# Transposes of the mixed rows: made in the second gather stage instead of the combination stage

## The chip, the cores and the metric

The kernel runs on one core of one Trainium2 chip. The metric is the device time of one execution in microseconds (us); less is better. Three executions of the kernel before took 3115.58, 3129.86 and 3129.86 us, median 3129.86 us.

## What is computed

A graph of 6250 nodes with 256 features and 100,000 edges goes through two layers; everything is float32. The parts that matter here, cut from the reference:

```python
# layer 0, end: two of six experts per node, weighted and added
x = x + ffn0(layernorm(x))                 # h = relu(..), sum over the two chosen experts of weight * expert(h)
xn = layernorm(x)                          # "the mixed rows": one mean and one deviation per node
# layer 1: messages over the edges, and a linear attention over all nodes
s      = xn[edge_src]                      # gather of rows, one per edge
msg    = tensor_product(s, edge_attr) * radial(edge_len_emb)
agg    = segment_sum(msg, edge_dst)        # sums per target node
qkv    = xn @ Wqkv.T                       # 8 heads of 64
k, v   = inst_norm(k), inst_norm(v)        # over the 64 features of a head
dots   = einsum("bhnd,bhne->bhde", k, v)   # summed over all 6250 nodes
mixed  = (q @ dots / n) @ Wout.T + bout
x = x + agg + mixed
x = layer1_ffn(x)                          # then the last stage
```

## The kernel before

The program is a row of phases, each between barriers of all engines. Each engine (PE, which multiplies matrices; DVE, ACT and POOL for vector work; SP, which only issues DMAs) has an instruction list of its own, written out by Python in a fixed order; waits on semaphores tie them together. Two phases are touched.

**The combination stage** (phase p6, second half, about 1575 to 1682 us of the span). The outputs of the experts lie in DRAM (`z_d`, two rows for each node). For each of `NB` = 25 blocks of 250 nodes (two tiles of 125 rows, t = 0 and 1) SP loads four pieces of `z_d` (500 KB in all: four DMAs from `start_rows`, L101). POOL multiplies the first expert's two tiles by their gates (L2082) and adds the residual `x1s` (L2085). DVE adds the second expert's product (`mix`, L2120), takes the statistics (L1468 to L1474), and from ACT's square root (`deviation_of`, L2012) makes reciprocal and shift (`shift_of`, L2130 and L2133). ACT writes the normed rows `xm` in four instructions (`normed`, L2002). SP stores them to `xm_d` (two DMAs, 250 KB). PE then transposes them (`turned`, four matmuls, L2061), ACT copies the result out of PSUM (`copy`, L2008), and SP stores it to `xmT_d` (250 KB, L1967). `pipeline` gives each stage function a lag: in step s an engine does the function of lag k for block s - k, in the order in which the list names them. ACT's list is

```python
pipeline(e, NB, [(copy, 2), (normed, 1), (deviation_of, 0)], loop=False)
```

**The second gather stage** (phase g2, from about 1682 to 2720 us) has 391 groups of 256 edges. For each, POOL issues two indirect DMAs of 128 rows from `xm_d` (`gather`, L2510) into a ring of `GB` = 13 groups; it waits until PE has summed the group that used the slot before. DVE and ACT make one-hot matrices, weighted per edge (`make_hot`, `weigh`). PE multiplies (`sums`, L2157) into PSUM, and DVE adds the PSUM result to a ring of node sums (`accumulate`, L2640). Up to group `ALONE` = 228 two groups share one PSUM bank, and the pairs take the banks 0, 1 and 4 in turn (`bank_of`). `timeline` orders all work by steps: step s has group s on POOL, group s - 5 on PE and so on. Other plans are laid over the groups: `KV` starts every fourth step from step 6, once for each of `NT` = 50 tiles of 125 nodes, and makes keys and values from `xmT_d` (`load_kv` on SP, `project` on PE L2763, `square` on ACT, `size` and `scale_k` on DVE, `products` on PE L2772); `MIX` folds the result into one matrix; `P9` and `F3`, from step 218, read `xmT_d` and the node sums to make the output rows of each tile (`product` and `turned` on PE, `x3_of` and `f3_of` on DVE). `RAD` makes the radial weights in 96 units (PE L2741 and L2753).

`Steps.wait(e, i, name)` makes engine e wait until item i has passed its step `name`; `Landing.wait` does so for DMAs. The other lines named in this document are helpers: L101 is `start_rows`, L1468 to L1474 `row_stats`.

## Time and profile before

| | |
|---|---|
| median of three runs | 3129.86 us (3115.58 to 3129.86) |
| the profiled execution | 3123.76 us |
| its span, first to last instruction | 3122.2 us |
| busy share of the span | PE 85%, POOL 58%, DVE 55%, ACT 46% |
| granted TensorE clock, mean | 0.943 of full speed |

The span is the profiled one; the profiled execution's own time is 1.6 us longer than it. All rows below come from that execution. Times in a row are counted from the span's start. A lower busy share than 100% says little by itself here: each stage has its own limit, so stages are read one by one.

### The profile page before, as it was taken

The numbers are of one execution on the slowest core, as the hardware profiler recorded it, in microseconds if no ns is written. First come the engines' busy times: TensorE is split into PE (matmuls) and PEld (weight loads), VectorE is DVE, ScalarE is ACT, GpSimd is POOL, SyncE is SP. The second block draws the span as 40 slices with busy tenths as digits, with TensorE's granted clock in tenths as the row PEclk, the third lists the DMA queues.
The fourth block names the chain that finished last, engine by engine and source line by source line (L and its number), as shares of the span: only waits on it lengthen the run. The fifth ranks groups of instructions, "written<-read, shape, count | busy, mean of one in ns | idle before, by whom it ended". The sixth has DMA issues, their size and how long they took to land. (4 is left out here: it accounts for less than half of the span.)

```text
span 3122.2 us, 54248 instructions
## 1 busy us (share of the span) xinstructions
PE 2645.5 (85%) x14909; PEld 2211.8 (71%) x14909; DVE 1716.8 (55%) x5340; ACT 1446.5 (46%) x4046; POOL 1819.7 (58%) x1962
## 2 busy tenths in 40 slices
PE   1999998998998996899934899899887888689998
PEld 1777778787887885788822666666677777578886
DVE  7733335777775667333364556566566667533333
ACT  4022222552233553333346988787576766322221
POOL 5777777777773355244476777777777777200000
PEclk9999999999999998899955999999999999799999
DMA  7364446767774774333276444444466655422222
GB/s 225 114 191 142 137 139 190 226 214 221 219 229 138 227 225 153 89 95 95 85 217 212 116 126 116 125 117 124 124 181 177 174 161 162 131 73 73 68 66 55
DMA packets 291701, 464.78 MB, mean 149 GB/s; under 512 B 91221, under 2 KB 224276, under 8 KB 290074
## 3 DMA queue, kind: packets, MB, share of 16 engines
q1 hardware_dynamic: 207804, 232.37, 25.1%
q0 software_dynamic: 81216, 221.98, 24.3%
q10 hardware_dynamic: 2402, 7.19, 0.7%
q8 instruction: 115, 1.88, 0.2%
q14 instruction: 164, 1.34, 0.1%
HBM read 349.16 MB, written 112.23 MB: 148 GB/s over the span
## 5 line engine op out<-in xcount | busy, mean ns | idle before, releaser
L2510 POOL DMA_INDIRECT g_got<-xm_d,idx x782 | 762.7, 975 | 253.5 <-issue 216.4
L886 POOL DMA_INDIRECT g_got<-xn_d,idx x702 | 684.8, 975 | 231.7 <-issue 211.9
L2157 PEld LDWEIGHTS ps<-g_hotw,g_got 128*128 128x128 f32 x3128 | 401.1, 196 | 168.8 <-DMA g_got<-xm_d,idx 89.0
L2157 PE MATMUL ps<-g_hotw,g_got 128*128 128x128 f32 (+11 forms) x3128 | 423.1, 285 | 95.9 <-DMA g_got<-xm_d,idx 66.6
L1279 PEld LDWEIGHTS ps<-g_hot,g_got 128*128 128x128 f32 x2808 | 354.0, 195 | 79.3 <-DMA g_got<-xn_d,idx 39.4
L1279 PE MATMUL ps<-g_hot,g_got 128*128 128x120 f32 (+4 forms) x2808 | 369.3, 279 | 34.2 <-DMA g_got<-xn_d,idx 26.5
L2559 ACT ACTIVATE g_hotw<-g_hot,g_wr 128x16 f32<-128x16 f32 (+8 forms) x1308 | 300.3, 308 | 86.7 <-DVE g_hot L598 86.4
L1479 POOL TENSOR_TENSOR p_ln_rs<-p_ln_pre,neg_half 125x2 f32<-125x2 f32 x50 | 35.2, 705 | 510.3 <-DVE p_ln_pre L1474 510.3
L2640 DVE TENSOR_TENSOR g_ring<-g_ring,ps 128x84 f32 (+10 forms) x391 | 133.5, 341 | 308.1 <-PE ps L2157 170.2
L2073 POOL DMA_INDIRECT z_d<-p_yj,p_to x108 | 122.1, 1130 | 205.7 <-DVE p_to L2106 183.8
L2960 ACT ACTIVATE p_hid<-ps,p_b 128x250 f32<-128x250 f32 x200 | 82.9, 466 | 278.5 <-PE ps L2922 278.5
L2037 PE MATMUL ps<-gin_hid,p_wj 128*128 128x256 f32 x864 | 197.4, 382 | 1.3 <-ACT gin_hid L1979 0.8
L2939 PE MATMUL ps<-p_w,p_hid 128*125 128x256 f32 x800 | 179.2, 382 | 22.2 <-ACT p_hid L2960 22.2
L1688 PE MATMUL ps<-gin_w,gin_hid 128*125 128x256 f32 x800 | 188.6, 385 | 9.1 <-POOL p_before L1747 9.1
L1418 PE MATMUL ps<-g_hT,g_w 128*128 128x250 f32 x800 | 190.8, 383 | 4.6 <-DVE g_hT L1105 4.6
L1093 DVE TENSOR_TENSOR g_ring<-g_ring,ps 128x40 f32 (+9 forms) x351 | 74.0, 211 | 217.0 <-PE ps L1279 125.4
L2922 PE MATMUL ps<-p_f3T,p_w 128*128 128x250 f32 x800 | 175.0, 375 | 12.8 <-DMA p_w<-in_L_ffn_W 12.8
L2939 PEld LDWEIGHTS ps<-p_w,p_hid 128*125 128x125 f32 x800 | 148.2, 188 | 52.9 <-ACT p_hid L2960 30.2
L2763 PE MATMUL ps<-g_half 128*125 128x512 f32 x400 | 184.9, 606 | 0.0
L2037 PEld LDWEIGHTS ps<-gin_hid,p_wj 128*128 128x128 f32 x864 | 165.1, 191 | 24.5 <-issue 1.1
L1988 ACT ACTIVATE gin_hid<-ps,p_wj 128x256 f32<-128x256 f32 x216 | 90.7, 471 | 188.6 <-PE ps L2037 188.6
L2922 PEld LDWEIGHTS ps<-p_f3T,p_w 128*128 128x128 f32 x800 | 151.3, 189 | 32.5 <-issue 12.9
(376 smaller groups left out, 5039.7 us busy)
## 6 DMA issues: line engine op xcount, KB each, us to landing
h_d<-gin_hid SPq DMA_DIRECT2D x23, 1000.0 KB
gin_hid<-h_d SPq DMA_DIRECT2D x23, 1000.0 KB
p_xr<-jobs_d SPq DMA_DIRECT2D x54, 258.0 KB, 2.8
g_got<-xm_d,idx POOLq DMA_INDIRECT x782
g_half<-xmT_d SPq DMA_DIRECT2D x100, 125.0 KB
g_got<-xn_d,idx POOLq DMA_INDIRECT x702
p_wj<-z_d SPq DMA_DIRECT2D x50, 224.0 KB
q_d<-g_qo SPq DMA_DIRECT2D x25, 250.0 KB
```

Of the source, the lines that this page charges most:

```text
L886: landed.start(e.indirect_dma_start(got[:, k % (2 * GB), :], None, xn_d[0:N, :], bass.IndirectOffsetOnAxis(ap=idx[:, HT + k:HT + k + 1], a ...
L1279: mm = e.matmul(to, got[:, 2 * (g % GB) + j, c * P:(c + 1) * P], hot[:, g % HR, j, 0:w].unsqueeze(1).broadcast_to([P, r, w]), start=(j == ...
L1418: mm = e.matmul(ps[:, 5 + n % 2, k * BN:(k + 1) * BN], w1[:, c, f:f + P], hT[:, i % 2, c, :], start=(c == 0), stop=(c == DC - 1))
L1688: mm = e.matmul(ps[0:TN, i % 2, t * D:(t + 1) * D], hid[:, slot(i), c, t * TN:(t + 1) * TN], w2[:, c, :], start=(c == 0), stop=(c == HC - 1))
L2037: mm = e.matmul(ps[:, 2 * k + u, o * JOB:(o + 1) * JOB], w[:, c, o * P:(o + 1) * P], src[:, u, c, :], start=(c == 0), stop=(c == DC - 1))
L2157: mm = e.matmul(to, rows[j][:, c * P:(c + 1) * P], hotw[:, j, c * w:4 * w].unsqueeze(1).broadcast_to([P, r, n]), start=(j == 0), stop=(j = ...
L2510: landed.start(e.indirect_dma_start(got[:, 2 * (g % GB) + j, :], None, xm_d[0:N, :], bass.IndirectOffsetOnAxis(ap=idx[:, 2 * g + j:2 * g + ...
L2559: ins = e.activation(hotw[:, u, 1, m * w:(m + 1) * w], hot[:, u, 1, 0:w], ACT.Copy, scale=chunk(n)[:, k, m:m + 1])
L2640: added.done(e.tensor_tensor(to, to, sums_of(bank_of(g)[0], w, bank_of(g)[1]), ALU.add), "add")
L2763: mm = e.matmul(ps[0:TN, bank, :], kT[:, i % 2, c, :], wkv[:, c, at:at + INNER], start=(c == 0), stop=(c == DC - 1))
L2922: mm = e.matmul(ps[:, q, m * BN:(m + 1) * BN], w1[:, k, c, f * P:(f + 1) * P], f3T[:, u, :, c * TN:(c + 1) * TN], start=(c == 0), stop=(c ...
L2939: mm = e.matmul(ps[0:TN, 4 + u, t * D:(t + 1) * D], hid[:, u, k, f, t * TN:(t + 1) * TN], w2[:, k, f, :], start=(j == 0), stop=(j == 2 * F ...
```

## The change

In the combination stage PE's `turned`, ACT's `copy` and SP's `store_T` go away, with their buffer and waits. ACT takes one of POOL's two gate products (`gate_first`, tile t = 0), and ACT's functions get larger lags. In the second gather stage a key and value step first loads the 125 rows of a tile from `xm_d` into `kr` (two slots that lie in `mix1`, which is written only later), PE transposes them (`turn_k`, into PSUM bank `XT` = 4), DVE copies them to `kT` (`copy_k`), and SP stores `kT` to `xmT_d` for the later readers (`store_kT`). All later steps of `KV` get two steps more of lag, `MIX` begins two steps later, and the shared banks are 0 and 1 only.

```diff
@@ combination stage
-                    pipeline(e, NB, [(load_z, 0), (store, ZB - 1), (store_T, ZB)], loop=False)
+                    pipeline(e, NB, [(load_z, 0), (store, ZB - 1)], loop=False)
...
-                        mturn.wait(e, i - AB, "turn")
                         m_out.wait(e, r, i // AB - 1)
...
-                    def copy(i, u, h):
-                        mturn.wait(e, i, "turn")
-                        t_out.wait(e, i % AB, i // AB - 1)
-                        mcopied.done(e.activation(xmT[:, i % AB, :], ps[:, 6 + u, 0:2 * BN], ACT.Copy), "T")
+                    def gate_first(i, u, h):
+                        z_in.wait(e, i % ZB, i // ZB)
+                        gated.done(e.activation(acc[:, i % AB, 0, :], z[:, i % ZB, 0, 0, :], ACT.Copy,
+                                                scale=gates[:, 2 * i, 0:1]), "g0")
...
-                    pipeline(e, NB, [(copy, 2), (normed, 1), (deviation_of, 0)], loop=False)
+                    pipeline(e, NB, [(normed, 3), (deviation_of, 2), (gate_first, 0)], loop=False)
...
-                    def turned(i, u, h):
-                        ln.norm.wait(e, i, "v1")
-                        mcopied.wait(e, i - 2, "T")
...
-                    pipeline(e, NB, [(turned, 0)], loop=False)
...
-                        for t in range(2):
-                            first.done(e.tensor_scalar(acc[:, i % AB, t, :], z[:, i % ZB, 0, t, :],
-                                                       gates[:, 2 * i + t, 0:1], None, ALU.mult), f"g{t}")
+                        first.done(e.tensor_scalar(acc[:, i % AB, 1, :], z[:, i % ZB, 0, 1, :],
+                                                   gates[:, 2 * i + 1, 0:1], None, ALU.mult), "g1")
                         first.wait(e, i, "g1")
+                        gated.wait(e, i, "g0")
@@ second gather stage
+            kr = mix1[0:TN, :, :]
...
-            MIX = [KV[-1] + 13]
+            MIX = [KV[-1] + 15]
...
-                return (FREE[g % 4], 0) if g >= ALONE else ((0, 1, 4)[g // 2 % 3], g % 2 * D)
+                return (FREE[g % 4], 0) if g >= ALONE else (g // 2 % 2, g % 2 * D)
...
                     def load_kv(i):
-                        proj.wait(e, i - 2, "v")
-                        k_in.start(e.dma_start(kT[:, i % 2, :, :],
-                                               xmT_d[i // 2].rearrange("p (c t n) -> p c t n", c=DC, t=2)[:, :, i % 2, :]),
-                                   i % 2)
+                        kturn.wait(e, i - 2, "T")
+                        k_in.start(e.dma_start(kr[:, i % 2, :], tile_of(xm_d, i)), i % 2)
+
+                    def store_kT(i):
+                        kcopy.wait(e, i, "T")
+                        k_out.start(e.dma_start(xmT_d[i // 2].rearrange("p (c t n) -> p c t n", c=DC, t=2)[:, :, i % 2, :],
+                                                kT[:, i % 2, :, :]), i % 2)
...
-  SP    (KV, [(load_kv, 0)])
+  SP    (KV, [(store_kT, 4), (load_kv, 0)])
-  ACT   (KV, [(square, 5), (roots, 8)])
+  ACT   (KV, [(square, 7), (roots, 10)])
-  DVE   (KV, [(scale_k, 9), (size, 6)])
+  DVE   (KV, [(scale_k, 11), (size, 8), (copy_k, 3)])
-  PE    (KV, [(products, 11), (project, 3)])
+  PE    (KV, [(products, 13), (project, 5), (turn_k, 2)])
...
+                    def copy_k(i):
+                        kturn.wait(e, i, "T")
+                        proj.wait(e, i - 2, "v")
+                        k_out.wait(e, i % 2, i // 2 - 1)
+                        kcopy.done(e.tensor_copy(kT[:, i % 2, :, :], ps[:, XT, 0:DC * TN].rearrange("p (c n) -> p c n", c=DC)), "T")
...
+                    def turn_k(i):
+                        k_in.wait(e, i % 2, i // 2)
+                        kcopy.wait(e, i - 1, "T")
+                        for c in range(DC):
+                            mm = e.transpose(ps[:, XT, c * TN:(c + 1) * TN], kr[:, i % 2, c * P:(c + 1) * P], ident[0:TN, 0:TN])
+                        kturn.done(mm, "T")
```

The four lines that begin with an engine's name are cut from the `timeline` calls. `project` waits for `kcopy` of its tile where it waited for `k_in`. SP's first `load` of `P9` also waits for the last stores of `kT`.

How the instructions stand now, at three places. First ACT in the middle of the combination stage, one block and the start of the next, before (`p_dev` is the square root, `p_xm` the normed rows, `p_xmT` the copy of the transposes):

```order
893 L2012 ACTIVATE p_dev<-p_ln_pre 125x2
894 L2008 ACTIVATE p_xmT<-ps 128x500
895 L2002 ACTIVATE p_xm<-p_acc,p_shift,xm_rs 125x64
896 L2002 ACTIVATE p_xm<-p_acc,p_shift,xm_rs 125x64x3
897 L2002 ACTIVATE p_xm<-p_acc,p_shift,xm_rs 125x64
898 L2002 ACTIVATE p_xm<-p_acc,p_shift,xm_rs 125x64x3
```

and ACT there in the changed kernel (L1998 is `gate_first`):

```order
889 L2003 ACTIVATE p_dev<-p_ln_pre 125x2
890 L1998 ACTIVATE p_acc<-p_wj,gates 125x256
891 L1993 ACTIVATE p_xm<-p_acc,p_shift,xm_rs 125x64
892 L1993 ACTIVATE p_xm<-p_acc,p_shift,xm_rs 125x64x3
893 L1993 ACTIVATE p_xm<-p_acc,p_shift,xm_rs 125x64
894 L1993 ACTIVATE p_xm<-p_acc,p_shift,xm_rs 125x64x3
```

The copy, which waits for PE, has given its place to a product that waits only for a DMA. Second, PE in the second gather stage, one key and value step in steady running, before (each `x2` of `ps<-g_hotw,g_got` is half of a group's sums; L2772 `products`, L2763 `project`):

```order
1220 L2753 MATMUL ps<-g_w1b,g_embT 128x512
1221 L2741 MATMUL ps<-ident,g_emb 80x128
1222 L2157 MATMUL ps<-g_hotw,g_got 128x128 x2
1223 L2157 MATMUL ps<-g_hotw,g_got 128x120 x2
1224 L2772 MATMUL ps<-g_half 128x128 x4
1225 L2763 MATMUL ps<-g_half 125x512 x4
1226 L2157 MATMUL ps<-g_hotw,g_got 128x128 x2
```

and PE in the changed kernel (L2752 is `turn_k`, L2771 and L2762 are `products` and `project`):

```order
1198 L2771 MATMUL ps<-g_half 128x128 x4
1199 L2762 MATMUL ps<-g_half 125x512 x4
1200 L2135 MATMUL ps<-g_hotw,g_got 128x128 x2
1201 L2135 MATMUL ps<-g_hotw,g_got 128x120 x2
1202 L2752 MATMUL ps<-ident,g_mix 128x125 x2
1203 L2135 MATMUL ps<-g_hotw,g_got 128x128 x2
1204 L2135 MATMUL ps<-g_hotw,g_got 128x120 x2
```

Two transposes stand behind a group's sums, one step after `project` of the tile before. Third, SP in the second gather stage, before:

```order
973 L588 DMA g_emb<-in_edge_attr 128x1280
974 L2468 DMA g_half<-xmT_d 128x2x125 x16
975 L588 DMA g_emb<-in_edge_attr 128x1280
976 L2468 DMA g_half<-xmT_d 128x2x125 x16
977 L588 DMA g_emb<-in_edge_attr 128x1280
```

and SP in the changed kernel (L2449 is `load_kv`, L2453 `store_kT`):

```order
970 L2449 DMA g_mix<-xm_d 125x256
971 L588 DMA g_emb<-in_edge_attr 128x1280
972 L2453 DMA xmT_d<-g_half 256x1x125
973 L2449 DMA g_mix<-xm_d 125x256
974 L2453 DMA xmT_d<-g_half 256x1x125
975 L2449 DMA g_mix<-xm_d 125x256
```

Each load now stands behind the store of the tile before, which waits for DVE's copy; before, the loads waited only for `project` two tiles back.

## Rows read from the trace of the kernel before

**Rows 1.** Page: the chain that ended last by engine, and a costliest group.

```profile
issue 16%; PE 12%; POOL 7%; DVE 5%; DMA 2%; DVEq 2%; ACT 1%; SPq 0%; POOLq 0%; ACTq 0%
...
L2510 POOL DMA_INDIRECT g_got<-xm_d,idx x782 | 762.7, 975 | 253.5 <-issue 216.4
```

**Rows 2.** Tile g_got: durations ns min/median/max, first and last start.

```profile
L2510 POOL DMA_INDIRECT g_got<-xm_d,idx x782: 942/949/2623, 1682.5 to 2682.4; - x196
```

**Rows 3.** Waits of POOL, 1700 to 2200 us: total, times, longest.

```profile
POOL g_got L2510 <- issue: 112.5, 369, 0.3
POOL g_got L2510 <- PE ps L2157: 7.0, 23, 0.3
```

**Rows 4.** Tile g_got from 1682 to 2495 us, POOL and PE.

```profile
L2510 POOL DMA_INDIRECT g_got<-xm_d,idx x635: 942/949/2623, 1682.5 to 2494.8; - x159
...
L2157 PE MATMUL ps<-g_hotw,g_got x2448: 232/275/582, 1693.5 to 2494.1; 128*128 128x96 f32 x47, 128*128 128x128 f32 x37, 128*128 128x120 f32 x27, 128*128 128x108 f32 x22
```

**Rows 5.** Timeline of the combination stage: start, length, instruction, idle before.

```profile
1587.78 1.85 ACT L2002 ACTIVATE p_xm<-p_acc,p_shift,xm_rs 125x64 f32<-125x64 f32 x4 [1.25 <-DVE p_shift L2133]
...
1589.57 1.09 DVE L2120 SCALAR_TENSOR_TENSOR p_acc<-p_wj,gates,p_acc 125x256 f32<-125x256 f32 x2
...
1592.10 0.72 DVE L1474 TENSOR_SCALAR p_ln_pre<-xm_mv 125x2 f32<-125x2 f32 x1
...
1626.48 1.85 ACT L2002 ACTIVATE p_xm<-p_acc,p_shift,xm_rs 125x64 f32<-125x64 f32 x4
...
1626.94 2.09 SPq L101 DMA_DIRECT2D p_wj<-z_d  x4
...
1628.38 1.09 PE L2061 MATMUL ps<-ident,p_xm 125*128 125x125 f32 x4 [2.42 <-ACT p_xm L2002]
...
1629.51 0.59 ACT L2008 ACTIVATE p_xmT<-ps 128x500 f32<-128x500 f32 x1 [0.68 <-PE ps L2061]
...
1629.99 1.85 ACT L2002 ACTIVATE p_xm<-p_acc,p_shift,xm_rs 125x64 f32<-125x64 f32 x4
...
1669.44 0.17 DVE L1474 TENSOR_SCALAR p_ln_pre<-xm_mv 125x2 f32<-125x2 f32 x1
...
1672.96 1.84 ACT L2002 ACTIVATE p_xm<-p_acc,p_shift,xm_rs 125x64 f32<-125x64 f32 x4
1674.83 0.79 SPq L101 DMA_DIRECT2D xm_d<-p_xm  x2
...
1675.66 1.28 SPq L1967 DMA_DIRECT2D xmT_d<-p_xmT  x2
```

**Rows 6.** Tile p_acc: POOL's product and sum.

```profile
L2082 POOL TENSOR_SCALAR p_acc<-p_wj,gates x50: 918/927/1223, 1579.8 to 1664.8; 125x256 f32<-125x256 f32 x50
...
L2085 POOL TENSOR_TENSOR p_acc<-p_acc,store x25: 1261/1265/1277, 1581.7 to 1665.9; 125x512 f32<-125x512 f32 x25
```

**Rows 7.** Window of the stage: busy us, then clock, DMA share, GB/s.

```profile
1620.00:1640.00 20.00, 6.01 (x23) 4.08 (x24) 16.16 (x48) 13.43 (x34) 17.95 (x18) 0.50 0.94 291
```

**Rows 8.** Tile g_gw: ACT, 125x256 with a scale per row.

```profile
L949 ACT ACTIVATE g_gw<-g_wn,ones,g_rr x50: 584/590/602, 518.3 to 959.6; 125x256 f32<-125x256 f32 x50
```

**Rows 9.** PE in 1700 to 2200 us, by line: busy, mean ns, idle before.

```profile
L2157 PE MATMUL ps<-g_hotw,g_got 128*128 128x96 f32 (+5 forms) x1593 | 204.4, 278 | 35.8 <-DMA g_got<-xm_d,idx 32.5 <-ACT g_hotw L2559 3.0
```

**Rows 10.** Chain at 1750 to 1759 us, a transpose in PE's row.

```profile
1758.63 0.11 PE ps L2741
```

**Rows 11.** DMA issues: KB each, us to landing.

```profile
f3T_d<-g_f3T SPq DMA_DIRECT2D x50, 125.0 KB, 4.0
```

**Rows 12.** Timeline of the second gather stage: gathers beside two DVE instructions.

```profile
1695.94 2.29 DVE L2593 SCALAR_TENSOR_TENSOR g_half<-g_means,g_half 128x2048 f32<-128x2048 f32 x1
1696.43 2.62 POOL L2510 DMA_INDIRECT g_got<-xm_d,idx  x1 [0.30 <-issue]
...
2232.94 1.23 DVE L2676 COPY g_a<-ps 128x1024 f32<-128x1024 f32 x1 [4.35 <-PE ps L2780]
2233.26 0.95 POOL L2510 DMA_INDIRECT g_got<-xm_d,idx  x1 [0.30 <-issue]
```

More of the change, by code:

```diff
@@ L1930, in gps_kernel @@
             ysum = ph.steps("ysum", "y")
-            first = ph.steps("first", "g0", "g1", "a")
+            gated = ph.steps("gated", "g0")
+            first = ph.steps("first", "g1", "a")
             mixed = ph.steps("mixed", "b0", "b1")
@@ L2391, in gps_kernel @@
             folded = ph.steps("folded", "pad")
-            k_in = ph.landing("k", 2)
+            k_in, k_out = ph.landing("k", 2), ph.landing("kT", 2)
+            kturn = ph.steps("kturn", "T")
+            kcopy = ph.steps("kcopy", "T")
             proj = ph.steps("proj", "k", "v")
@@ L2483, in load @@
                             dots.wait(e, NT - 1, "dots")
+                            for u in range(2):
+                                k_out.wait(e, u, (NT - 1 - u) // 2)
                         rows.wait(e, i - XI, "rows")
@@ L2574, in _ @@
                     timeline(LAST_STEP, (GROUPS, [(weigh, 3)]), (RAD, [(do_silu, 7), (copy_emb, 3)]), (ZERO, [(zero, 0)]),
-                             (KV, [(square, 5), (roots, 8)]), (PAIRS, [(deviations, 9)]), (F3, [(copy, 2)]))
+                             (KV, [(square, 7), (roots, 10)]), (PAIRS, [(deviations, 9)]), (F3, [(copy, 2)]))
                 @block.vector
```

27 lines of the change are left out of this document (5 added, 22 removed).

## The prediction

> **What bounds the kernel now.** I read the chain that ended last first. It shares 16% to "issue", 12% to PE and 7% to POOL [rows 1], so no engine holds the whole kernel and each stage has to be read alone. The change touches two stages, the combination stage and the second gather stage.
>
> The second gather stage is bound by POOL's gathers. POOL issues 782 of them from 1682.5 to 2682.4 us [rows 2], one every (2682.4 - 1682.5) / 781 = 1.28 us: 0.975 us for the DMA instruction itself, and a gap that "issue" explains nearly always [rows 1]. From 1700 to 2200 us POOL waited for PE 23 times, never over 0.3 us, which is also the gap of a gather that waits for nobody [rows 3]. The reader should see in this that POOL never stalls there. The ring holds 13 groups, and POOL stalls only when PE is 13 groups behind. How near that comes is seen from two counts at one time: at 2495 us POOL had issued 635 gathers, 317.5 groups, and PE had finished 2448 / 8 = 306 groups (eight records for each), so PE was 11.5 groups behind [rows 4]. That is near the tightest place, with 1.5 groups of room, 1.5 x 2.56 = 3.8 us. So work that is added for PE, DVE or ACT in this stage costs nothing until PE falls 13 groups behind, and the stage as a whole moves with POOL's first gather.
>
> POOL's first gather comes when the combination stage has ended and its rows have landed. So each microsecond that the combination stage loses is lost from the total.
>
> That stage has a period for each block of 250 rows. ACT's first normed block begins at 1587.78 us, its 25th at 1672.96 [rows 5]: 85.18 / 24 = 3.55 us. What ends the period is a loop between ACT and PE that nothing overlaps: ACT norms (1.85 us), PE transposes what was just written (1.09 us and the way to it), ACT copies (0.59 us), and norms again, 1626.48 to 1629.99 us, 3.51 us [rows 5]. POOL is close behind with two products and a sum, 2 x 0.93 + 1.27 = 3.13 us [rows 6], and so is the DMA: its share was 0.94 at 291 GB/s [rows 7], so it is busy for 0.94 x 3.53 = 3.3 us of each block. Three resources at 3.1 to 3.5 us is why one edit alone could not have gained much here; the change relieves all three.
>
> **The change, term by term.**
>
> *The period of the combination stage.* After the change the limits for a block are these.
> - ACT: norms 1.85 us [rows 5], square root 0.20 (estimate, a 125x2 instruction), one product of 125x256 with a scale per row, 0.59 us [rows 8], and about 0.1 of gaps: 2.7 us.
> - POOL: 0.93 + 1.27 us [rows 6]: 2.2, with gaps 2.3 us.
> - DVE: from the start of the second product, 1589.57, to the start of the last small instruction, 1592.10, are 2.53 us [rows 5], plus that instruction. It took 0.17 us with POOL idle and 0.72 with POOL at work [rows 5]. So 2.70 to 3.25 us.
> - DMA: 750 of 1000 KB stay (two reads of 250 KB and one write; a second write goes). By bytes 3.3 x 0.75 = 2.5 us, and at the same 0.94 share 2.65.
> - SP: four loads took 2.09 us to issue and two stores 0.79 [rows 5]: 2.9 us. This was hidden under 3.5; now it is among the longest.
> - A loop over two blocks: ACT's product, POOL's sum 1.27, DVE's product pair 1.09, reciprocal and shift about 0.45, ACT's norms 1.85, square root 0.20, ACT's next product 0.59, and six hand-overs of about 0.03: 5.6 / 2 = 2.8 us.
>
> ACT now waits for `z_d` itself, with the norms of an earlier block queued behind it. The loads of block i + 1 stand on SP behind the store of block i - 4: 0.79 + 2.09 us of issue, 2.5 to 4 us to land (the nearest row, a 125 KB store, says 4.0 [rows 11]), product 0.6, norms 1.9, over three blocks: 2.6 to 3.1 us. I take 2.9 us, at SP's own time and in the middle of the last loop. Gain 24 x (3.55 - 2.9) = 15.6 us. The ends are 2.7 us (20.4) and 3.26 (7.0), if DVE is held up in every block.
>
> On DVE's small instruction a rule bears. The row says that it lasted 0.72 us beside POOL and 0.17 without. The Trainium skill (SBUF — State Buffer, section "SBUF: two separate sides") says that VectorE and GpSimd share a port pair as an exclusive lock held for a whole instruction, in place of each sharing the bandwidth. By that rule the small instruction ends when POOL's sum ends, whereupon DVE's next product may start anyway, and the period follows the loop's 2.8 us; by the row at its worst it would be 3.25.
>
> *The start of that stage.* POOL makes one product of 0.93 us [rows 6] for a block where it made two. ACT's first norms stand behind the sums of two blocks: 2 x 0.93 = 1.9 us earlier.
>
> *Its end.* The last norms end at 1674.80. The last issue of SP ends at 1675.66 + 1.28 = 1676.94 now, and at 1674.83 + 0.79 = 1675.62 without the transposed rows [rows 5]: 1.3 us. What follows (landing, barrier, loads) is unchanged.
>
> *Transposes in the second gather stage.* Two for each of 50 tiles. A transpose in a row of matmuls advances the chain by 0.11 us [rows 10], so 0.22 us per tile. A tile takes four groups, 4 x 2.56 = 10.2 us of POOL's time, 49 tiles in 1700 to 2200 us: 10.8 us of new work, and PE's idle time before the sums alone was 35.8 us there [rows 9]. Even at the 0.278 us of one whole matmul record in that row it would be 27 us, still less. Cost 0. In the combination stage the granted clock is 0.50 already [rows 7], so PE's idling there loses nothing new.
>
> *`copy_k` on DVE.* The nearest row is a copy out of PSUM of 1024 columns in 1.23 us [rows 12]; by columns 0.30 us for 250, 15 us in all, against 1.23 each (61 us) as the upper bound. DVE mostly waits for PE in this stage. Cost 0. It could hurt POOL instead: one DVE instruction with both inputs in SBUF stretched the gather beside it to 2.62 us, whereas the gather beside the copy out of PSUM took its usual 0.95 [rows 12]. I take the second, 0; the first is a rival below.
>
> *The load and store of each tile.* 125 KB in and 125 KB out, every 10.2 us. Each load now waits for the copy of the tile before. From PE's transposes the way is: copy 0.3, SP's two issues 0.8, landing up to 4.0 [rows 11], transposes 0.2: some 5.5 us of 10.2. SP has nothing else but three large loads of `g_emb` in this stretch; a load behind one of them may be late by some us, which PE's room takes. Cost 0.
>
> *Two shared banks for three.* A pair's bank is wanted again three steps after its last sum, and DVE's two additions stand one step before. PE has 2 steps of about 2.5 us, DVE needs under 1 us. Cost 0.
>
> *`P9` two steps later.* The first 27 tiles come later, the 28th by one step, the rest at their old steps. The dense part ends one step later, at the tight place of rows 4. With 3.8 us of room I put 1 us of stall there, between 0 and 5.
>
> **Sum.** 15.6 + 1.9 + 1.3 - 1 = 17.8 us off. The profiled execution's own time was 3123.8 us, 6.1 under the median of the three runs: 3106 us.
>
> **The rivals.**
> - *The forecast*, a gain of 14 to 24 us: 0.60, of which 0.02 at the low end count as within 0.5%.
> - *The combination stage is held by what stays* (SP's issue, loads that land late, DVE behind POOL), period 3.1 to 3.4 us: 24 x 0.3 + 3.2 - 1 = 9 us off, 3114 us. For it speaks that three loops lie within 0.3 us of each other, against it that each one by itself fits in 2.9. 0.23.
> - *The copies stretch gathers.* If each of the 50 held up a gather for its own 0.3 to 0.43 us, 15 to 21 us come back: 3121 to 3127 us. Rows 12 speak against it. 0.07.
> - *The transposing loop outlasts four groups* (the slower side). Copy, store, load, landing and transposes have 10.2 us. Each tile's excess is counted 50 times: 0.36 us eats the gain, and from 0.67 us, a loop of 10.9 us, the kernel is slower by over 0.5%; at 12 us it is 90 us, less 33 us that the ring's room takes, less 18: 3163 us. The in-order queues speak for it (SP's load behind a wait for DVE, DVE's copy behind a wait for PE), the 5.5 us against. 0.10.
>
> About 0.5%, 16 us, is what a measurement of this kernel can tell from no change; the three runs before lie 14 us apart. Faster by more: 0.58. Within: 0.02 + 0.23 + 0.07 = 0.32. Slower: 0.10.
>
> The range goes down to 3094: a gain of 23 us at the 2.7 us period, and 7 us of scatter of the runs. It goes up to 3124, which takes in the second rival, and most of the third. What is left out is the slower rival and the far ends: 2 in 10.
>
> **What the profile would show.** Starts of ACT's norms 2.9 us apart, and the first gather at about 1664 in place of 1682.5. POOL's gathers still 1.28 us apart, with no wait over 0.3 us, and the last one 1000 us after the first. A transpose pair in the second gather stage that adds 0.2 us to PE's row, with waits for the load of `kr` rare. The prediction is wrong if norms come over 3.2 us apart, if gathers beside `copy_k` last longer than 0.95 us, or if POOL waits for PE's sums from 1700 us on.

## The result and the profile after

The changed kernel takes 3111.06 us (median of 20 runs, 3103.31 to 3116.28), the kernel before 3123.59 us on the same chip (20 runs, 3114.24 to 3129.86). The ratio is 0.996, with a 95% interval of 0.995 to 0.997: 12.5 us less. The prediction was 3106 us, in a range of 3094 to 3124. Two later executions, of 3718 us (e4) and 5550 us (e8), were in a slower state and are left out of all medians. The profiled execution of the changed kernel took 3110.37 us, its span is 3108.8; rows of before are those of its profiled execution, span 3122.2.

The page first: the chain that ended last by engine, and the costliest group (busy, mean ns of one, idle before).

```profile
issue 16%; PE 12%; DVE 6%; POOL 6%; DVEq 2%; DMA 2%; ACT 1%; SPq 0%; POOLq 0%; ACTq 0%
...
L2496 POOL DMA_INDIRECT g_got<-xm_d,idx x782 | 763.9, 977 | 250.7 <-issue 215.7
```

It reads like [rows 1]; at this scale nothing has changed. The gathers of the second gather stage, with the tile's durations, first and last start, and the sums that follow them:

```profile
L2135 PE MATMUL ps<-g_hotw,g_got x3128: 232/275/609, 1674.4 to 2685.4; 128*128 128x128 f32 x62, 128*128 128x96 f32 x38, 128*128 128x176 f32 x20, 128*128 128x80 f32 x19
...
L2496 POOL DMA_INDIRECT g_got<-xm_d,idx x782: 942/946/2846, 1664.1 to 2664.9; - x196
```

The first gather is at 1664.1 us (forecast about 1664; 1682.5 in [rows 2]). From first to last are 1000.8 us, against 999.9. POOL's waits in the stretch that [rows 3] has, moved with the stage (1681 to 2182 us; total, times, longest):

```profile
POOL g_got L2496 <- issue: 111.5, 366, 0.3
POOL g_got L2496 <- PE ps L2135: 7.9, 26, 0.3
```

No wait is over 0.3 us, so POOL never stalls here either. The transposes and their copy, by line in the same stretch:

```profile
L2638 DVE COPY g_half<-ps 128x250 f32<-128x250 f32 x49 | 20.5, 418 | 59.0 <-PE ps L2752 58.9
L2752 PE MATMUL ps<-ident,g_mix 125*128 125x125 f32 x98 | 18.5, 270 | 0.0
```

49 tiles cost PE 18.5 us (0.38 a tile: forecast 0.22, with 0.28 a transpose as the upper bound) and DVE 20.5 (0.42 a tile, forecast 0.30). PE never stood idle ahead of a transpose, so the load of `kr` was never late there.

The combination stage, as a timeline (start, length, engine, idle before):

```profile
1584.47 1.86 ACT L1993 ACTIVATE p_xm<-p_acc,p_shift,xm_rs 125x64 f32<-125x64 f32 x4 [1.46 <-DVE p_shift L2111]
...
1586.78 1.86 ACT L1993 ACTIVATE p_xm<-p_acc,p_shift,xm_rs 125x64 f32<-125x64 f32 x4
...
1590.47 1.86 ACT L1993 ACTIVATE p_xm<-p_acc,p_shift,xm_rs 125x64 f32<-125x64 f32 x4 [1.46 <-DVE p_shift L2111]
...
1607.44 0.49 ACT L1998 ACTIVATE p_acc<-p_wj,gates 125x256 f32<-125x256 f32 x1
...
1608.08 1.26 POOL L2063 TENSOR_TENSOR p_acc<-p_acc,store 125x512 f32<-125x512 f32 x1 [0.15 <-ACT p_acc L1998]
1608.26 1.10 DVE L2111 SCALAR_TENSOR_TENSOR p_shift<-xm_mv,xm_rs 125x2 f32<-125x2 f32 x1
...
1609.40 1.87 ACT L1993 ACTIVATE p_xm<-p_acc,p_shift,xm_rs 125x64 f32<-125x64 f32 x4 [1.46 <-DVE p_shift L2111]
...
1611.69 0.16 DVE L2111 SCALAR_TENSOR_TENSOR p_shift<-xm_mv,xm_rs 125x2 f32<-125x2 f32 x1
...
1654.91 1.86 ACT L1993 ACTIVATE p_xm<-p_acc,p_shift,xm_rs 125x64 f32<-125x64 f32 x4 [0.44 <-DVE p_shift L2111]
```

The 25 norms start from 1584.47 to 1654.91: 70.44 / 24 = 2.94 us each, where [rows 5] gave 3.55. They don't come evenly: 2.31 and 3.69 us lie between the first three. The shift of 125x2 lasts 0.16 us alone, but at 1608.26, beside POOL's sum, 1.10; ACT's norm waits behind it. The sum ends at 1609.34, the shift at 1609.36.

The waits of that stage (1573 to 1662 us) name four suspects for the 2.94 us, the loads ahead of POOL and of ACT, the shift, and ACT's product:

```profile
POOL p_acc L2059 <- DMA p_wj<-z_d: 16.6, 17, 6.0
ACT p_acc L1998 <- DMA p_wj<-z_d: 16.6, 10, 11.7
ACT p_xm L1993 <- DVE p_shift L2111: 12.5, 19, 1.6
...
POOL p_acc L2063 <- ACT p_acc L1998: 5.0, 7, 1.5
```

Most turns go by the loads. One round of that loop, from ACT's norms of one block over SP's store and its next load (that of the block five later) to ACT's product of that block and the norms behind it:

```profile
1611.88 1.87 ACT L1993 ACTIVATE p_xm<-p_acc,p_shift,xm_rs 125x64 f32<-125x64 f32 x4 [0.26 <-DVE p_shift L2111]
...
1613.93 0.82 SPq L101 DMA_DIRECT2D xm_d<-p_xm  x2
...
1614.79 1.80 SPq L101 DMA_DIRECT2D p_wj<-z_d  x4
...
1619.80 0.51 ACT L1998 ACTIVATE p_acc<-p_wj,gates 125x256 f32<-125x256 f32 x1 [0.39 <-DMA p_wj<-z_d]
...
1620.44 1.85 ACT L1993 ACTIVATE p_xm<-p_acc,p_shift,xm_rs 125x64 f32<-125x64 f32 x4
```

The norms at its end are those of the block three later: 8.56 / 3 = 2.85 us a block. The next round, from the norms at 1614.34 to those at 1623.49 us, takes 3.05 a block. ACT's norms wait 1.4 us or more for the shift in only 4 of the 24 turns.

The window (busy us of PE, PEld, DVE, ACT, POOL; granted clock, DMA share, GB/s) shows none of them full. DVE comes nearest with 18.24 of 20 us, in which the time that it is held is counted. The DMA fell from the 0.94 and 291 of [rows 7]:

```profile
1620.00:1640.00 20.00, 0.00 (x0) 0.00 (x0) 18.24 (x63) 16.81 (x42) 16.26 (x14) 0.50 0.90 267
```

**Where the time came from.** From the first load of `z_d` to the first gather are 91.2 us (1572.85 to 1664.09), against 107.0 (1575.52 to 1682.53): 15.8 us less. Of these 14.7 are the period (85.2 less 70.4 us), 0.6 the start (load to first norm 11.6, against 12.3), 0.4 the end (last norm to first gather 9.2, against 9.6). The stages ahead ended 2.7 us earlier, which the change doesn't touch. Against this stand 1.0 us in the gathers and 4.1 us from the last gather to the end of the span (443.9, against 439.8). 15.8 + 2.7 - 1.0 - 4.1 = 13.4 us, the difference of the two spans. The medians, which don't hold the scatter of one execution, give 12.5.

### The profile page after: what moved, and what is told of

Same layout as the page of the kernel before. It is cut to its first block and busy times, and to the rows that moved or that the text cites. A ratio compares the mean times of both kernels' runs of the same rounds, so it can differ in the third digit from the quotient of the medians.

```text
span 3108.8 us, 54377 instructions
## 1 busy us (share of the span) xinstructions
PE 2628.5 (85%) x14909; PEld 2210.4 (71%) x14909; DVE 1731.9 (56%) x5390; ACT 1451.0 (47%) x4048; POOL 1794.1 (58%) x1937
## 5 line engine op out<-in xcount | busy, mean ns | idle before, releaser
L2496 POOL DMA_INDIRECT g_got<-xm_d,idx x782 | 763.9, 977 | 250.7 <-issue 215.7
L2921 PE MATMUL ps<-p_f3T,p_w 128*128 128x250 f32 x800 | 175.2, 375 | 13.4 <-DMA p_w<-in_L_ffn_W 13.4
L2762 PE MATMUL ps<-g_half 128*125 128x512 f32 x400 | 184.0, 603 | 0.0
L1980 ACT ACTIVATE gin_hid<-ps,p_wj 128x256 f32<-128x256 f32 x216 | 90.7, 471 | 188.3 <-PE ps L2028 188.3
```

The lines of the kernel that those rows point to most:

```text
L2496: landed.start(e.indirect_dma_start(got[:, 2 * (g % GB) + j, :], None, xm_d[0:N, :], bass.IndirectOffsetOnAxis(ap=idx[:, 2 * g + j:2 * g + ...
L2762: mm = e.matmul(ps[0:TN, bank, :], kT[:, i % 2, c, :], wkv[:, c, at:at + INNER], start=(c == 0), stop=(c == DC - 1))
L2921: mm = e.matmul(ps[:, q, m * BN:(m + 1) * BN], w1[:, k, c, f * P:(f + 1) * P], f3T[:, u, :, c * TN:(c + 1) * TN], start=(c == 0), stop=(c ...
```

## The experiments

The runs of this part fell on four other chips. On these every kernel is slower: the kernel before takes 3584 us on chip B, 3549 on C, 3551 on D and E (A is the chip above). So each kernel is compared with the kernel before on its own chip, and that chip's trace says what is different. "PE sets the pace" stands in the expectations for chips B to E, where POOL is seen to pause; the last part says how much of this was true.

| kernel | chip | median us | ratio to before (95%) | norm period | `z_d` load to first gather | first to last gather | ring waits |
|---|---|---|---|---|---|---|---|
| before | A | 3123.6 | | 3.55 | 107.0 | 999.9 | 0 |
| after | A | 3111.1 | 0.996 (0.995 to 0.997) | 2.94 | 91.2 | 1000.8 | 0 |
| e1_gate_only | B | 3581.5 | 0.9991 (0.9977 to 1.0006) | 3.51 | 106.1 | 1227.2 | 11 |
| e2_copy_later | B | 3578.5 | 0.999 (0.9977 to 1.0002) | 3.38 | 103.9 | 1227.7 | 10 |
| e3_no_gate | B | 3593.9 | 1.0038 (1.0024 to 1.0052) | 3.21 | 98.5 | 1238.5 | 16 |
| e4_store_later | B | 3581.3 | 0.9993 (0.9975 to 1.001) | 2.96 | 90.7 | 1242.9 | 17 |
| e5_both | C | 3576.5 | 1.0076 (1.0053 to 1.0098) | 3.52 | 106.6 | 1222.3 | 19 |
| e7_two_banks | C | 3564.4 | 1.0039 (1.0023 to 1.0055) | 3.59 | 108.5 | 1226.2 | 15 |
| e8_split_sum | C | 3543.9 | 0.9982 (0.9966 to 0.9998) | 2.77 | 85.8 | 1228.8 | 16 |
| e9_after_again | C | 3550.3 | 1.0004 (0.9991 to 1.0018) | 2.90 | 90.5 | 1227.3 | 17 |
| e10_bank_shared | D | 3547.8 | 0.9981 (0.9965 to 0.9998) | 2.85 | 89.2 | 1220.2 | 12 |
| e11_best | D | 3539.1 | 0.9964 (0.9948 to 0.998) | 2.75 | 85.6 | 1216.0 | 11 |
| e12_before_again | D | 3557.2, one run | | 3.54 | 107.7 | 1209.7 | 8 |
| e13_best_again | E | 3536.8 | 0.9949 (0.9931 to 0.9967) | 2.66 | 84.3 | 1217.3 | 14 |

The period is the last start of ACT's norms less the first, by 24. The fifth to seventh number are from each kernel's one profiled execution. A ring wait is a gap of POOL over 0.45 us ahead of a group's first gather that ends within 1 us of PE's last sum for the group 13 before, counted in the trace. The stages ahead, whose code is the same in all, scatter too: on one chip the combination stage begins up to 16 us earlier in one execution than in another (1776.8 us in e7, 1792.7 in e8). So a total can't be made up from the stages of one execution.

**The combination stage: what held it before, what holds it now.** The first four kernels were to tell this.

`e1_gate_only`: the kernel before, with Scalar's product added.

```diff
+                    def gate_first(i, u, h): ...   # as in the change, POOL keeps one product
-                    pipeline(e, NB, [(copy, 2), (normed, 1), (deviation_of, 0)], loop=False)
+                    pipeline(e, NB, [(copy, 4), (normed, 3), (deviation_of, 2), (gate_first, 0)], loop=False)
```

> The kernel before with only the gate product moved to ACT; the transposes, ACT's copy and the store of the transposed rows stay in the combination stage. The product stands behind the square root, in the time in which ACT waits for PE (1.18 us, of which 0.2 are used). Theory (the loop of norms, transposes and copy sets the period of 3.55 us): the starts of the norms stay 3.5 us apart and the time is that of before within 3 us. Rival (POOL's two products and a sum, or the z loads, set it): 3.2 to 3.3 us apart and 5 to 8 us faster. The second gather stage is that of before: its length from the first gather to the end is one more sample of what before gives (1439.6 us).

The period stays at 3.51 us in every block, though POOL has 0.93 us less to do. Its timeline:

```profile
1831.42 1.10 PE L2067 MATMUL ps<-ident,p_xm 125*128 125x125 f32 x4 [2.42 <-ACT p_xm L2003]
1832.55 0.59 ACT L2009 ACTIVATE p_xmT<-ps 128x500 f32<-128x500 f32 x1 [0.82 <-PE ps L2067]
1833.03 1.84 ACT L2003 ACTIVATE p_xm<-p_acc,p_shift,xm_rs 125x64 f32<-125x64 f32 x4
...
1834.93 1.10 PE L2067 MATMUL ps<-ident,p_xm 125*128 125x125 f32 x4 [2.42 <-ACT p_xm L2003]
```

Norm, transpose, copy, norm: 1831.42 to 1834.93 is one turn of the loop, 3.51 us, and the added product lies in ACT's wait. The loop that the prediction named is the bound of before; the next run opens it.

`e2_copy_later`: the kernel before, with the copy one block later, so that ACT norms a block while PE transposes the last.

```diff
-                    pipeline(e, NB, [(copy, 2), (normed, 1), (deviation_of, 0)], loop=False)
+                    pipeline(e, NB, [(copy, 3), (normed, 1), (deviation_of, 0)], loop=False)
```

> The kernel before with one number changed: ACT copies the transposes one block later (lag 3 in place of 2), so that it no longer waits for PE. All the work and all the bytes stay. Theory (that loop sets the period, POOL at 3.25 and the DMA at 3.3 us are next): norms 3.25 to 3.35 us apart, 5 to 7 us faster than before. Rival (the DMA at a share of 0.94 is already the limit): no change. From the first gather to the end 1439.6 us as before, if this stretch does not scatter.

The period falls to 3.38 us, mostly 3.1 to 3.6 from block to block, where 3.25 to 3.35 was expected. The transfers are next: from 1835 to 1855 us the DMA share is 0.98 at 302 GB/s, and at that rate the 1.02 MB of a block take 3.4 us. By this sum the transposes could not have stayed at 2.94. The kernel that would test it, this edit together with Scalar's product, was not run.

`e3_no_gate`: the kernel after, with both products on POOL.

```diff
-                        first.done(e.tensor_scalar(acc[:, i % AB, 1, :], z[:, i % ZB, 0, 1, :], ...), "g1")
+                        for t in range(2):
+                            first.done(e.tensor_scalar(acc[:, i % AB, t, :], z[:, i % ZB, 0, t, :], ...), f"g{t}")
-                    pipeline(e, NB, [(normed, 3), (deviation_of, 2), (gate_first, 0)], loop=False)
+                    pipeline(e, NB, [(normed, 1), (deviation_of, 0)], loop=False)
```

> The changed kernel with both gate products on POOL again; the transposes stay in the second gather stage. Theory (POOL is then the longest, 0.93 + 0.93 + 1.27 and gaps): norms 3.2 to 3.3 us apart, so about 7 us of the changed kernel's gain are lost, some 5 to 6 us faster than before. Rival (what holds the changed kernel at 2.93 us is the loads and not the engines, and the product on ACT is worth nothing): norms 2.9 to 3.0 us apart, 12 us faster. From the first gather to the end: 1444.7 us in the changed kernel's profile against 1439.6 before; if the 5 us belong to the moved transposes this run shows 1443 or more, if they are scatter it can show 1440.

The period is 3.26 us in nearly every block, and POOL has no gap in it:

```profile
1832.46 1.26 POOL L2057 TENSOR_TENSOR p_acc<-p_acc,store 125x512 f32<-125x512 f32 x1
1833.70 1.94 POOL L2054 TENSOR_SCALAR p_acc<-p_wj,gates 125x256 f32<-125x256 f32 x2
...
1835.72 1.27 POOL L2057 TENSOR_TENSOR p_acc<-p_acc,store 125x512 f32<-125x512 f32 x1
```

So the move of the transposes alone gives 0.3 us a block, and Scalar's product the other 0.3. Neither gives 0.6 alone (e1: 0.03). The time missed its expectation: in place of 5 to 6 us faster, this kernel is 0.38% slower than before (0.24 to 0.52%). What it loses in the second gather stage is taken up below.

`e4_store_later`: the kernel after, with SP's store behind one more load, which gives the loads of a block more time.

```diff
-                    pipeline(e, NB, [(load_z, 0), (store, ZB - 1)], loop=False)
+                    pipeline(e, NB, [(load_z, 0), (store, ZB)], loop=False)
```

> The changed kernel with SP's store of the mixed rows one block later, so that each load of z stands ahead of one store more that waits for ACT's norms. Theory (the loop over SP: norms, store, load, landing, product holds the period at 2.93 us, with spacings that alternate from 2.3 to 4.2): norms 2.6 to 2.75 us apart, 4 to 7 us faster than the changed kernel, 17 to 19 us than before, waits of ACT and POOL for the z loads nearly gone. Rival (DMA share 0.9 is the limit): 2.9 us apart, no change against the changed kernel.

Behind the first block all waits for the loads are gone. What is left from 1805 to 1870 us:

```profile
ACT p_xm L1993 <- DVE p_shift L2111: 16.7, 12, 1.6
POOL p_acc L2063 <- ACT p_acc L1998: 16.2, 13, 1.8
```

and the period is what it was, 2.96 us, now nearly all in turns of 2.31 and 3.68. The 2.6 to 2.75 us that I expected did not come. This doesn't clear the loads in the kernel after, where POOL waits for them 17 times; it shows that a second limit of nearly the same length stands right behind them. The timeline shows that one:

```profile
1841.72 1.26 POOL L2063 TENSOR_TENSOR p_acc<-p_acc,store 125x512 f32<-125x512 f32 x1
1841.91 1.09 DVE L2111 SCALAR_TENSOR_TENSOR p_shift<-xm_mv,xm_rs 125x2 f32<-125x2 f32 x1
...
1843.03 1.86 ACT L1993 ACTIVATE p_xm<-p_acc,p_shift,xm_rs 125x64 f32<-125x64 f32 x4 [1.46 <-DVE p_shift L2111]
...
1845.15 0.16 DVE L2111 SCALAR_TENSOR_TENSOR p_shift<-xm_mv,xm_rs 125x2 f32<-125x2 f32 x1
...
1845.41 1.26 POOL L2063 TENSOR_TENSOR p_acc<-p_acc,store 125x512 f32<-125x512 f32 x1 [1.53 <-ACT p_acc L1998]
```

In every second block DVE's shift starts just behind POOL's sum and lasts as long as that does. ACT, which waits for the shift, comes late to its next product, and POOL's next sum waits for that product. From one sum to the next that way is 1841.72 to 1845.41, the 3.69 us of the long turn: held shift 1.3, norms 1.86, product 0.49. With the shift free the turn takes 2.31. The two together are the prediction's loop over two blocks, 5.6 us by its sum and 5.99 measured. Here ACT's norms wait 1.4 us or more for the shift in 11 of the 24 turns; in the kernel after it is 4, and 2 in e9, which has the same stage. That the loop over the loads and this one come out at nearly the same period is chance.

`e8_split_sum`: both limits relieved. The kernel after, the store as in e4, and POOL's sum in two, so that each is shorter and one stands ahead of the wait for Scalar.

```diff
                         first.wait(e, i, "g1")
+                        first.done(e.tensor_tensor(acc[:, i % AB, 1, :], acc[:, i % AB, 1, :],
+                                                   x1s[:, 2 * i + 1, :], ALU.add), "a1")
                         gated.wait(e, i, "g0")
-                        first.done(e.tensor_tensor(acc[:, i % AB, :, :], acc[:, i % AB, :, :],
-                                                   x1s[:, 2 * i:2 * i + 2, :], ALU.add), "a")
+                        first.done(e.tensor_tensor(acc[:, i % AB, 0, :], acc[:, i % AB, 0, :],
+                                                   x1s[:, 2 * i, :], ALU.add), "a")
```

> The kernel after with POOL's sum over two tiles split in two (the one for its own product made at once, the other when Scalar's product is there), and the store one step later on SP. Theory: the period of 2.94 us is held by a loop over two blocks that contains POOL's sum of 1.26 us, and by DVE's shift, which lasts 1.1 us when it meets that sum; a sum of 0.65 us shortens both, so the period comes to 2.6 to 2.75 us and the stage ends 4 to 8 us earlier than in the kernel after (ratio to it 0.998). Rival: the period is DMA or SP's issue; then it stays at 2.9 us. If two short locks meet DVE as often as a long one, it stays too.

The norms now come every 2.64 us in 15 of the 24 steps, 2.77 on the mean (2.75 and 2.66 in the two later runs). The tile of the shift: durations in ns, minimum, median, maximum.

```profile
L2113 DVE SCALAR_TENSOR_TENSOR p_shift<-xm_mv,xm_rs x25: 160/491/565, 1803.3 to 1870.0; 125x2 f32<-125x2 f32 x25
```

Its longest is 0.57 us, where the kernel after had 1.20 (1.10 on this chip). The stage is 4.7 us shorter than in the unchanged kernel after on the same chip (85.8, against 90.5 us). The median is 6.3 us lower; by the ratios it is 0.22%, with an uncertainty of about as much. The split sum without the later store was not run, so the share of each edit is not known. What holds the turns of 2.64 us now is POOL. The window from 1806 to 1822 us (as above) and POOL's work for one block in it:

```profile
1806.00:1822.00 16.00, 0.00 (x0) 0.00 (x0) 14.71 (x55) 13.40 (x37) 15.50 (x19) 0.50 0.90 262
...
1815.00 0.92 POOL L2059 TENSOR_SCALAR p_acc<-p_wj,gates 125x256 f32<-125x256 f32 x1
1816.01 0.97 POOL L2062 TENSOR_TENSOR p_acc<-p_acc,store 125x256 f32<-125x256 f32 x1
1816.94 0.72 POOL L2065 TENSOR_TENSOR p_acc<-p_acc,store 125x256 f32<-125x256 f32 x1
```

The two sums take 1.69 us where the whole one took 1.26, and with the product that is 2.61 of the 2.64 us. SP has no room left either: from its store at 1808.36 to that at 1819.23 us it issues without a wait, 2.72 us a block.

**The second gather stage: is what was put there free?** On chip A it was, to 1 us. On chip B, e3 and e4 gain 8 and 15 us against e1 in the combination stage and give them back: their gathers last 11 to 16 us longer than in e1 and e2, which keep the stage of before. This lies in the ring waits: their time beyond the usual gap is 32 and 30 us in e1 and e2, 46 and 49 in e3 and e4. Four kernels took the stage's edits apart.

`e7_two_banks` is the kernel before with one line of the change:

```diff
-                return (FREE[g % 4], 0) if g >= ALONE else ((0, 1, 4)[g // 2 % 3], g % 2 * D)
+                return (FREE[g % 4], 0) if g >= ALONE else (g // 2 % 2, g % 2 * D)
```

> The kernel before with only two shared PSUM banks for the early sums, nothing else. Theory: two banks cost nothing, first to last gather within 1 us of the kernel before on the same chip, ratio 1.000 within 0.001. Rival: with two banks PE waits for DVE's two additions at each pair of groups; then PE loses up to 0.3 us for each of some 100 pairs and, where PE sets the pace, 10 us or more show (ratio 1.003), and the transposes are free.

`e5_both` has the combination stage of before and the second gather stage of after, so that the transposes are made twice (in the first for nothing); `e9_after_again` is the kernel after.

> The combination stage of the kernel before with the second gather stage of the kernel after: the transposes are made in both. Theory: the second gather stage's part costs nothing where POOL's gathers set its pace (first to last gather 1000 us, ratio 1.000 within 0.001), and where PE sets it, its 50 tiles cost 11 to 16 us, 0.2 to 0.3 us of PE for each tile (ratio 1.003 to 1.0045). Rival: the part costs nothing on PE either and the 11 to 15 us seen between the kernels were the ending of the combination stage at another moment; then the ratio is 1.000 everywhere.

> The kernel after, unchanged, as the base for the other three on their chip. Where POOL sets the second gather stage's pace: ratio 0.996 to the kernel before. Where PE sets it: 16 us are gained in the combination stage and 11 to 16 lost in the second gather stage, ratio 0.998 to 1.001, as the run with the later store (0.9993) showed.

`e12_before_again` is the kernel before.

> The kernel before, unchanged, for its profile on the chip of these runs. Theory: first to last gather as in the run with three banks shared, norms every 3.51 to 3.55 us, and no waits of the sums for DVE's additions where PE sets the pace. Rival: its gather stage is as long as that of the kernels with two banks; then the time that these lose is elsewhere.

The two banks alone cost 0.39% (14 us, 8 to 20), with PE's work unchanged; here the rival held. No kernel with three banks was profiled on chip C, so where the 14 us are lost can only be read from PE's waits on two chips, from 1950 to 2700 us. The kernel before (e12, chip D):

```profile
PE ps L2157 <- issue: 52.5, 55, 2.6
```

With two banks (e7, chip C):

```profile
PE ps L2157 <- DVE g_ring L2640: 54.3, 19, 7.3
PE ps L2157 <- DVE g_hot L598: 49.6, 23, 4.4
```

The kernel after (e9, chip C):

```profile
PE ps L2135 <- DVE g_hot L598: 56.8, 30, 7.0
PE ps L2135 <- DVE g_ring L2626: 27.6, 13, 4.2
```

With three banks the sums in this stretch wait for nothing of DVE's. With two, they wait 104 and 84 us for its additions (`g_ring`) and for its one-hot matrices, which stand behind the additions in DVE's order. POOL's ring waits rise from 8 to 11 (e1, e2, e12) to 15 to 19 (all kernels with two banks). But these lines tell for whom PE waited last, and not what the banks cost: all of PE's idle time, from 30 us after the first gather to the last one, is 238 us in e12, 248 in e2 and 258 in e1, which have three banks, and 248 in e9 and 262 in e7, which have two. In the kernels with three banks much of it stands under "issue". So that two banks cost time is shown, and that they do it through DVE's order is likely.

What the transposes add is not settled. e5 is slower than e7 by 12 us at the medians, and slower than before by 0.76%, where 0.3 to 0.45% was expected. But e9's combination stage is 16 us shorter than e5's (90.5, against 106.6) and its median is 1.4 us over that of before, so that its second stage costs some 17 us by that count, where e5 says 27 (19 to 35). And from the first gather to the end of the span the profiled execution of e5 is no longer than that of e7 (1672.4, against 1673.6 us).

`e10_bank_shared`: the kernel after, with three banks for the sums, and the transposes in the bank of the keys.

```diff
-            XT, KB, V, DOTS = 4, 3, 5, 6
+            KB, V, DOTS = 3, 5, 6
+            XT = KB
-                return (FREE[g % 4], 0) if g >= ALONE else (g // 2 % 2, g % 2 * D)
+                return (FREE[g % 4], 0) if g >= ALONE else ((0, 1, 4)[g // 2 % 3], g % 2 * D)
 ...
+                        squares.wait(e, i - 1, "raw")        # in turn_k
-            MIX = [KV[-1] + 15]
+            MIX = [KV[-1] + 13]
-                             (KV, [(products, 13), (project, 5), (turn_k, 2)]), ...
+                             (KV, [(products, 11), (project, 4), (turn_k, 2)]), ...
```

with `square`, `roots`, `scale_k` and `size` back at their steps of before.

> The kernel after, but the early sums keep their three PSUM banks, and the transposes of a tile share bank 3 with its key result (project one step after copy_k instead of two, turn_k waits for the squares of the tile before; the dense part keeps its step of before). Theory: what the second gather stage loses where PE sets its pace is the third bank (waits of the sums for DVE, 73 to 104 us in 750 us with two banks, none with three), not the transposes. Then first to last gather returns to that of the kernel before within 3 us, no such waits, and the gain of the combination stage shows in the total: ratio 0.995. Where POOL sets the pace the ratio is 0.995 to 0.996 as well. Rival: the transposes and their copy on DVE cost it themselves; then the span stays 11 to 15 us longer and the ratio is 0.999 to 1.0. A second rival: with one bank for transposes and keys PE waits for Scalar's squares once per tile, and it is slower than the kernel before.

The largest waits of PE from 1950 to 2700 us:

```profile
PE ps L2135 <- issue: 30.2, 37, 1.9
PE ps L2754 <- ACT g_half L2520: 19.4, 12, 3.4
```

The sums' waits for DVE are gone, and a wait of the transposes for Scalar's squares is new, as the second rival said, but it came 12 times and not once per tile, and the kernel is not slower. The gathers last 1220.2 us, 10.5 more than in e12 on the same chip, so the transposes with their copy, load, store and waits cost something there even with three banks, as far as one execution of each can tell. They are 7 us shorter than in e9, but on another chip, and e1 and e12, whose second stage is the same, differ by 17.5 us from chip to chip. The ratio, 0.9981, lies between theory (0.995) and rival (0.999 to 1.0). It is 8 us better than e9's 1.0004, with an uncertainty as large: how much the third bank gave back is not shown.

`e11_best` is e10 with the split sum and the later store; `e13_best_again` is the same kernel.

> The kernel of the run before with POOL's split sum and the later store. Each gain adds to the other: 24 x 0.15 to 0.2 = 4 to 5 us less than that kernel, ratio to before 0.993 to 0.994. Rival: the combination stage's last 4 us lie behind something else, then the ratio equals that kernel's.

> The kernel with the split sum, the later store and three banks once more, as it is. If POOL sets the pace of the second gather stage on this chip (first to last gather near 1000 us): norms every 2.7 to 2.8 us, ratio to before 0.993 to 0.995, and the time from the last gather to the end tells of the 4 us that the kernel after lost there: 440 us if the dense part's later steps were the reason, 444 us if they were not. If PE sets the pace (near 1215 us): ratio 0.995 to 0.998, as on the other such chip.

They take 3539.1 us on chip D (12.3 less than before there) and 3536.8 on E (13.9 less): ratios 0.9964 and 0.9949. The gain of e11 was to be 0.6 to 0.7% and is 0.36% (0.20 to 0.52). The kernel after showed no gain on C and, with the later store, none on B. So this version is faster than before on both chips, where the kernel after was not on its two; the two kernels were never run on the same chip, and on chip A, where POOL doesn't pause, this one was not run at all. Chip E pauses like the other three, so e13 can't tell of the 4 us at the end of the gathers, for which it was also run.

## Why the prediction was right, and where not

- *Direction, size and range*: right. The forecast was 17.8 us off, of which 12.5 came; the range held.
- *The bound of the combination stage before* (the loop of ACT and PE, 3.51 us): shown by e1, where POOL had less to do and nothing moved, and e2, where the loop was opened and the period fell.
- *Its period after*, 2.9 us for a gain of 15.6: measured 2.94 and 14.7. I took it "at SP's own time and in the middle of the last loop", that is from SP and the landing of loads. The loop over the loads is there in most turns, with 2.85 and 3.05 us in the two rounds above, where I had 2.6 to 3.1. SP's own time was sized too large: its store and loads take 0.82 + 1.80 = 2.62 us, not 2.9, and SP waits 17.7 us for ACT's norms in the stage. It is a limit only in e8. What I missed is a second limit of the same length: the loop over two blocks (my 2.8) comes to 2.96 with DVE's shift held behind POOL's sum. It sets 4 of the 24 turns here, and every second one once e4 had taken the waits for the loads away. I had named the hold on DVE as a term for its own busy time ([rows 5], 0.72 us); it acts through ACT, which waits for the shift. So the number rests on the right loop for most turns, and that the other one does not make it longer is luck.
- *The two readings of [rows 5]*: the rule's was the better. The Trainium skill (SBUF — State Buffer, section "SBUF: two separate sides") has the port pair as an exclusive lock, held for a whole instruction. This trace agrees for POOL's sum: all five shifts that began during a sum ended 0.02 us after it (1609.36 and 1609.34 for one), and so did 12 of 12 in e4. So did the 13 small instructions of L1474 that began during one, though they read one tensor only. But beside POOL's product, which reads one tensor too, ten shifts lasted 0.16 to 0.24 us and ended 0.44 us ahead of the product; there the whole instruction was not waited for.
- *The start*, 1.9 us: 0.6. The saved products were there: counted from the first load of `z_d`, the first shift begins 1.56 us earlier (1583.27 less 1572.85, against 1587.50 less 1575.52). But it lasts 1.17 us beside POOL's sum, where before it lasted 0.24, and 0.6 is left.
- *The end*, 1.3 us: 0.4. The issues came as forecast: SP's last ends 2.7 us after the last norms' start (1657.59 less 1654.91), where it was 4.0. From there to the first gather it is 6.5 us now and was 5.6, so "what follows is unchanged" was the wrong half. The store of `xm_d` is now the last one, but that alone is not the reason: it is the last one in e4, e8 and e11 too, and there it is 5.6 to 5.7 us (6.5 in e3, e9, e10 and e13). The cause stays open.
- *Transposes, copy, load and store at no cost; no stretched gathers*: on chip A shown right. The gathers have a median of 0.946 us, beside `copy_k` too, and no gap of POOL between two of them is over 0.32 us. The stage lasts 1.0 us longer, but not by the stall at the tight place for which I had put down 1 us: the gathers themselves take 763.9 us in place of 762.7. That term was right by luck. The room of 3.8 us that I took from the count in [rows 4] was too large. At the closest, PE's sums ended 3.0 us ahead of the gather that reuses their slot before, and end 0.8 us ahead of it now. On chips B to E 0.8 us is also the least that is seen where POOL does wait, so once, at 2469 us, the reserve was used up.
- *Two banks at no cost*: right on chip A (from 1900 us on PE waits 17.6 us for `g_ring`, against 12.9), wrong on C. The step "PE has 2 steps of about 2.5 us, DVE needs under 1 us" counts DVE's own time, not its order. Where DVE is held up by something else, two banks bind PE to it within two steps; this fits the waits of e7, but was not tested by itself.
- *A term that was missing*: PE's lag at the end of the gathers. I let added work be free as long as POOL doesn't stall, but what PE is behind when the last gather is issued comes after it. The last sums end 20.8 us after the last gather began, against 15.8 before, and the end of the span comes 4.1 us later after it. This rests on one execution each. On chips B to E the time from last gather to end is 446.9 to 451.8 us for every kernel, of either kind, so it stays open how much of the 4 us is the change's.
- *The slower rival* (the transposing loop outlasts four groups) did not come. On chips B and C the gain is lost in the second gather stage, but not through that loop: PE waited for the load of `kr` once (1.7 us in e5) or not at all in the stretches read there.

## What to carry to other kernels

Work taken off the path gives time only until the next loop. Two limits of the same length hide each other: that nothing moves when one is taken away doesn't clear it, as e4 shows. Here it was two edits together, the transposes off PE's loop and a product off POOL, that made 0.6 us a block where one alone made 0.03 and the other 0.3. Work moved into "free" room of another stage uses up a reserve, here PE's distance to POOL and a PSUM bank: count what is left of it, and what is behind at the stage's end, since on a chip that has less of it the added work shows in the time. Where a small instruction of VectorE is waited for, look whether it lasts as long as a sum of GpSimd beside it (1.10 us in place of 0.16 here), and keep such sums away from it or cut them.

## What the runs showed of the hardware

The same kernel takes 3124 us on one chip and 3549 to 3584 on four others, at a mean granted clock of 0.943 and about 0.90. The clock is not enough to explain it: in the second gather stage all engines stop together for a time. From e9, the kernel after on chip C:

```profile
2157.43 0.95 POOL L2496 DMA_INDIRECT g_got<-xm_d,idx  x1 [0.30 <-issue]
...
2159.75 0.87 PE L2135 MATMUL ps<-g_hotw,g_got 128*128 128x96 f32 x6 [1.17 <-issue]
2159.95 0.60 ACT L2517 ACTIVATE g_half<-ps 125x512 f32<-125x512 f32 x1 [6.07 <-DMA h_d<-gin_hid]
2160.06 0.42 DVE L2638 COPY g_half<-ps 128x250 f32<-128x250 f32 x1 [3.76 <-remote]
...
2160.79 0.94 POOL L2496 DMA_INDIRECT g_got<-xm_d,idx  x1 [2.42 <-PE ps L2135]
```

POOL pauses like this some 100 times, by 2.1 us more than its usual gap of 0.3, about once for every four groups, and the releasers named by the profile differ from one engine to the next. In e12 only 8 of 100 such pauses ended with the sums that POOL could have waited for; they make 23 of 213 us (47 of 228 in e9). So "PE sets the pace" in my expectations was true of a tenth to a fifth of these gaps. The pauses are the whole difference in this stage: 213 us, where the gathers of e12 last 209.8 us longer than those of the kernel before on chip A. Another 214 us lie ahead of the combination stage (it begins at 1789.6 us, against 1575.5) and were not read. What stops the engines in the other gaps is not settled. No run tried it.
